# Memory and experts on one core: retrieval by the silu table, its first block in halves, other blocks' sums moved, a sorting router

## The chip, the cores and the metric

The kernel runs on one core of a Trainium2 chip, as one launch. The time is device microseconds from start to end of the execution; the input arrays lie in HBM before it and the output lies there after it.

## What is computed

The input x has 2048 tokens of 128 features, float32. Two sublayers follow, each with a layer norm around it. The first is a memory that is trained by one step and then read; the second is a mixture of eight experts of which each token uses two. Cut to what matters:

```python
def _lmm(params, h):
    for W, b in params:
        h = h + silu(h @ W + b)
    return h

# memory, on x = layernorm(x)
keys, queries, values = x @ Wk + bk, x @ Wq + bq, x @ Wv + bv
alr = 0.1 * sigmoid(x @ Wlr + blr)
grads = grad(sum(mean((_lmm(ps, keys) - values) ** 2, -1) * alr))(((W1, b1), (W2, b2)))
new = p * (1 - LR * WD) - LR * g / (sqrt(g * g) + EPS)
x1 = x0 + layernorm(_lmm(new, queries))

# experts, on y = layernorm(x1)
z = layernorm(y, g, b)
probs = softmax(z @ rW + rb)
w = probs of the top two, divided by their sum
hid = gelu(z @ W1[e] + b1[e])
out = x1 + layernorm(y + sum over e of w[e] * (hid @ W2[e] + b2[e]))
```

## The kernel before

The 2048 tokens are four blocks (NB) of 512, each of four tiles of 128 tokens. Every engine has its own program, written out by hand; they meet only in semaphores. There is no scheduler: the order in the code is the order on each engine.

**Gradients.** Five waves (`wave(w)`) take the blocks through keys, values, the two layers forward and back, and the two weight gradients, which accumulate in PSUM. The last wave also holds the four query products (`q_product`), all of them through PSUM bank 1, with `qT_out` on ScalarE copying each into `qT`. VectorE then makes the new weights and biases (`adam`): first `w2n` together with the biases `bn`, then `w1n`.

**Retrieval** (TensorE `rz1_product`, `rz2_product`, `r_transpose`, `z_transpose`; ScalarE `rsig1_out`, `rsig2_out`, `zT_out`; VectorE `retrieve1`, `retrieve2`, `norm_r`, `residual`, `norm_z`, `z_low`). A layer of the memory is a product, a sigmoid of it by ScalarE (with the bias), then on VectorE a product (matmul + bias) * sigmoid (L903, L911) and a sum with the layer's input (L907, L914). After two layers TensorE transposes the result to token-major form, VectorE takes its statistics, GpSimd the power -0.5 (`rsqrt`, L304), VectorE the residual x1 and the statistics of that, GpSimd two more powers, VectorE the normalised z, TensorE its transposes, and ScalarE the copies `zT` and `z_hi`. `z_hi` is a value in the reduced format that TensorE reads in one pass; `z_lo` is what is left of z, so that a product with three terms is accurate. Blocks 0 to 3 are interleaved; both layers of all four blocks come before the experts, norms only of block 0. Meanwhile `keep_clock` has TensorE transpose the identity into a spare bank 6, 8, 48 and 3 times.

**Experts.** The phase is a loop over slots, -2 to 31; slot m is block m // 8 and expert m % 8. In a slot TensorE makes the hidden products of slot m + 2 (`hidden`, six matmuls of 512 columns) and the output of slot m (`output`, eight matmuls of 128 columns that take two instructions each); ScalarE makes the gelus; VectorE multiplies the output with the router's weight and adds it (`add_expert`, L1063). `due(position, slot)` puts the norms, transposes and router of the next block into fixed slots of the block that runs. `b2_term` is a product of the transposed router weights with the experts' output biases, which GpSimd lays out in `b2_diag` (L320, L324); `start_sum` begins a block's sum with it.

**Router.** `logits` are four small products. VectorE adds the bias and subtracts the maximum (`shift_logits`), ScalarE takes the exponential, and `route` finds the top two by maxima, comparisons and a ramp that settles ties, makes the two weights (`w_tok`), and splits them into a high and a low part (`w_parts`), which `w_transpose` turns.

## Time and profile before

| | |
|---|---|
| Median of 3 runs | 196.87 us (196.78 to 197.1) |
| Profiled execution, own time | 196.74 us |
| Its span, first to last instruction | 194.6 us |
| Mean granted clock of TensorE | 0.984 |
| TensorE busy (matmuls) | 174.4 us, 90% |
| VectorE busy | 147.4 us, 76% |
| ScalarE busy | 102.7 us, 53% |
| GpSimd busy | 25.6 us, 13% |
| Chain that ended last, by engine | TensorE 72%, VectorE 21%, ScalarE 2%, issue 2%, DMA 2% |

The span runs from the first to the last instruction; the 2.1 us around it are the launch and end of the execution. Busy shares are averages over stages. The profile calls TensorE's matmuls PE and its weight loads PEld, VectorE DVE, ScalarE ACT, GpSimd POOL. A granted clock of 1.00 is 2.4 GHz, 0.50 is 1.2 GHz.

### The profile page before, as it was taken

To read this page: it belongs to the slowest core of one execution; us is meant where nothing else is said; L and a number is where in the kernel's file an instruction comes from. 1 tells how busy PE (TensorE), PEld (TensorE's weight loads), DVE (VectorE), ACT (ScalarE), POOL (GpSimd) and SP (SyncE) were. 2 spreads that over 40 slices of the span, in tenths; PEclk is the share of its full clock that TensorE was granted. 3 is DMA by queue.
4 is the path that set the end of the run, shared out by engine and by line. 5 is a ranking of instruction groups with operands and counts; after the bars stand their busy time and mean duration, and the time that the engine had idled before them with its cause. 6 is when DMAs were issued, how large, how long until landed. Compare 5 with 4: busy or idle time off the path is not lost.

```text
span 194.6 us, 3223 instructions
## 1 busy us (share of the span) xinstructions
PE 174.4 (90%) x1085; PEld 142.0 (73%) x1085; DVE 147.4 (76%) x562; ACT 102.7 (53%) x166; POOL 25.6 (13%) x33
## 2 busy tenths in 40 slices
PE   6499999999887994999999899999899999999950
PEld 6344465656543953899999799989789999999950
DVE  1989998997837999797348996568996567557384
ACT  3159768584442167635587336586346595535500
POOL 1450000000000291140000242001142000020011
PEclk9999999999999998899999999999999999999997
DMA  5990000000000000000000000100000100001001
GB/s 162 297 295 18 2 3 0 0 0 3 0 2 0 0 2 3 0 0 0 3 0 2 0 3 0 54 3 0 2 0 3 54 2 0 3 2 54 0 0 54
DMA packets 3423, 4.99 MB, mean 26 GB/s; under 512 B 336, under 2 KB 1744, under 8 KB 3408
## 3 DMA queue, kind: packets, MB, share of 16 engines
q1 hardware_dynamic: 3408, 4.81, 7.8%
q8 instruction: 8, 0.13, 0.3%
q14 instruction: 7, 0.06, 0.1%
HBM read 3.76 MB, written 1.05 MB: 25 GB/s over the span
## 4 chain that ended last, share of the span: by engine, by line
PE 72%; DVE 21%; ACT 2%; issue 2%; DMA 2%; DVEq 0%; ACTq 0%
PE bank L345 65%; PE bank L353 4%; DVE stats L769 3%; DMA x_tok<-in_x_dram 2%; DVE xnT L1063 2%; DVE mv L772 1%; DVE vT L914 1%; DVE s L903 1%; DVE s L911 1%; DVE xnT L907 1%; DVE xn_tok L782 1%; PE bank L476 1%; ACT s L597 1%; PE bank L488 1%; DVE xnT L1074 1%
## 5 line engine op out<-in xcount | busy, mean ns | idle before, releaser
L1063 DVE SCALAR_TENSOR_TENSOR xnT<-bank,w_tok,xnT 128x128 f32<-128x128 f32 x124 | 35.0, 345 | 25.6 <-PE bank L345 25.2
L304 POOL TENSOR_TENSOR rstd<-vpe,minus_half 128x4 f32<-128x4 f32 (+1 forms) x21 | 20.8, 997 | 164.6 <-DVE vpe L777 150.1
L345 PE MATMUL bank<-z_hi,fW_hi 128*128 128x512 f32 x64 | 28.3, 442 | 2.6 <-DVE z_lo L949 2.6
L345 PE MATMUL bank<-z_lo,fW_hi 128*128 128x512 f32 x64 | 25.6, 400 | 0.0
L345 PE MATMUL bank<-z_hi,fW_lo 128*128 128x512 f32 x64 | 25.5, 399 | 0.0
L345 PEld LDWEIGHTS bank<-fW_sb,sig 128*128 128x128 f32 x192 | 23.0, 192 | 0.8
L345 PE MATMUL bank<-fW_sb,sig 128*128 128x128 f32 x192 | 23.2, 275 | 0.0
L708 ACT ACTIVATE sig<-bank,early_sb 128x512 f32<-128x512 f32 x24 | 16.2, 688 | 12.5 <-PE bank L345 12.5
L345 PEld LDWEIGHTS bank<-fW_sb,k_tok 128*128 128x128 f32 x160 | 19.4, 192 | 0.8
L345 PEld LDWEIGHTS bank<-fW_sb,h1T 128*128 128x128 f32 x160 | 19.4, 192 | 0.8
L708 ACT ACTIVATE k_tok<-bank,early_sb 128x512 f32<-128x512 f32 x20 | 13.5, 687 | 12.2 <-PE bank L345 12.1
L345 PE MATMUL bank<-fW_sb,h1T 128*128 128x128 f32 x160 | 19.5, 275 | 0.0
L345 PE MATMUL bank<-fW_sb,k_tok 128*128 128x128 f32 x160 | 19.5, 275 | 0.0
L708 ACT ACTIVATE h1T<-bank,early_sb 128x512 f32<-128x512 f32 x20 | 13.5, 687 | 10.1 <-PE bank L345 10.0
L345 PEld LDWEIGHTS bank<-z_hi,fW_hi 128*128 128x128 f32 x64 | 12.6, 197 | 4.2 <-issue 2.7
L345 PEld LDWEIGHTS bank<-z_lo,fW_hi 128*128 128x128 f32 x64 | 12.3, 192 | 2.8
L424 PEld LDWEIGHTS bank<-ident 128*128 128x128 f32 x93 | 11.7, 153 | 3.1 <-issue 1.6
L424 PE MATMUL bank<-ident 128*128 128x128 f32 x93 | 12.3, 293 | 1.5 <-POOL ident L295 1.5
L345 PEld LDWEIGHTS bank<-z_hi,fW_lo 128*128 128x128 f32 x64 | 12.4, 194 | 1.5
L345 PE MATMUL bank<-xnT,early_sb 128*128 128x512 f32 x24 | 12.0, 596 | 0.8 <-ACT xnT L610 0.8
L597 ACT ACTIVATE s<-bank,bn 128x512 f32<-128x512 f32 x8 | 5.5, 687 | 11.0 <-PE bank L345 11.0
L345 PEld LDWEIGHTS bank<-xnT,early_sb 128*128 128x128 f32 x24 | 4.1, 190 | 3.9 <-issue 3.9
(133 smaller groups left out, 280.7 us busy)
## 6 DMA issues: line engine op xcount, KB each, us to landing
x_tok<-in_x_dram SPq DMA_DIRECT2D x4, 256.0 KB, 4.6
fW_raw<-in_fW_dram SPq DMA_DIRECT2D x1, 1024.0 KB, 9.4
out_dram<-xn_tok SPq DMA_DIRECT2D x3, 256.0 KB, 2.5
early_sb<-in_early_dram SPq DMA_DIRECT2D x1, 268.0 KB, 3.7
late_sb<-in_late_dram SPq DMA_DIRECT2D x1, 264.0 KB, 5.5
b_raw<-in_late_dram SPq DMA_DIRECT2D x16, 4.0 KB
out_dram<-xn_tok SPq DMA_DIRECT2D x2, 128.0 KB, 1.9
fW_sb<-in_fW_dram SPq DMA_DIRECT2D x1, 0.5 KB, 11.9
```

The lines of the kernel that those rows point to most:

```text
L304: pool.tensor_tensor(rstd[:, ln, where], vpe[:, ln, where], minus_half[:, 0:where.stop - where.start], ALU.pow).then_inc(rstd_ready[ln], 1)
L345: return pe.matmul(out_, lhsT, rhs, start=start, stop=stop)
L353: last = pe.transpose(bank[7][:, i * P:(i + 1) * P], pieces(i), ident[:])
L424: pe.transpose(bank[scratch][:, 0:P], ident[:], ident[:])
L476: last = pe.transpose(bank[4][:, i * P:(i + 1) * P], rT[:, b * BLOCK + i * P:b * BLOCK + (i + 1) * P], ident[:])
L488: last = pe.transpose(bank[7][:, i * P:(i + 1) * P], zt_tok[:, t, :], ident[:])
L597: act.activation(cut(into, b), source[:], ACT.Sigmoid, bias=bias).then_inc(s, 1)
L708: act.activation(g_buf[n % G_RING], bank[H_BANK[n % len(H_BANK)]][:], ACT.Gelu, bias=col(FB1 + n % UB)).then_inc(g_done, 1)
L769: last = dve.bn_stats(stats[:, t, :], source(i, t))
L772: last = dve.bn_aggr(mv[:, ln, t, :], stats[:, t, :])
L782: last = dve.tensor_scalar(into[:, t, :], source[:, t, :], mv[:, ln, t, 0:1], scale[:, t:t + 1], ALU.subtract, ALU.mult)
L1063: last = dve.scalar_tensor_tensor(out=y_tok[:, t, :], in0=bank[Y_BANK[m % len(Y_BANK)]][:, i * P:(i + 1) * P], scalar=w_tok[:, t, e:e + 1] ...
```

## The change

**Retrieval.** A layer's activation is one operation on ScalarE, Silu with the bias (`silu1`, `silu2`); VectorE keeps only the sums (`hidden_sum`, `retrieved_sum`). A one-element Silu (`warm`) stands ahead, which brings the table load with it. The retrieval works in five pieces (`RETRIEVED`): two halves of block 0, then blocks 1, 2 and 3. For blocks 1 to 3 the second layer doesn't wait for a sum: TensorE adds the two products w2n * query and w2n * silu in PSUM (`rz2_query`, `rz2_rest`). VectorE's sums for these blocks move into the expert phase, in slots -1, 7 and 15 (`R_SUM`), and with them the norms by two slots or so. Of the `keep_clock` calls behind the gradients only the one with 6 stays.

**Order.** Query products alternate between two banks. Adam makes the biases, `w1n`, then `w2n`. GpSimd builds `b2_diag` as soon as `w1n` is ready, in two operations instead of three. The first two hidden products are made together (`first_hidden`), with the low part of z last; the logits of block 0 follow them.

**Router.** VectorE's max gives the sorted logits of a tile, match_replace marks the top two in a padded copy, and a comparison turns the marks into 0.5 at two places. The weights of a top-two softmax are 0.5 * (1 + tanh((l - other) / 2)); VectorE makes the argument as l minus half the pair's sum, and ScalarE takes Tanh. The exponential, its reductions and the ramp are gone.

The diff, cut to its core:

```diff
         WARM_UP = 28
+        Q_BANK = (1, 2)
...
-        NORM_R, RESIDUAL, NORM_Z, Y_STATS, Y_NORM, Z_LOW, LOGITS_SHIFT, ROUTE = -2, -1, 0, 1, 2, 2, 4, (5, 6)
-        R_TR, Z_TR, LOGITS, EXP, W_TR, B2_TERM = -2, 2, 3, 5, 7, 8
+        R_SUM, NORM_R, RESIDUAL, NORM_Z, Y_STATS, Y_NORM, Z_LOW, CHOOSE, ROUTE = -1, 0, 1, 2, 2, 3, 4, 5, 6
+        R_TR, Z_TR, LOGITS, GATE, W_TR, B2_TERM = 0, 3, 4, 5, 7, 8
...
-        RZ1, RZ2 = (0, 1, 2, 0), (3, 5, 6, 2)
+        RETRIEVED = [(0, HALF), (HALF, HALF)] + [(TB * b, TB) for b in range(1, NB)]
+        RZ1, RZ2 = (3, 5, 7, 5, 6), (6, 2, 3, 2, 6)
+        R_BANK, Z_BANK = (4, 0, 4, 4, 4), (7, 1, 7, 7, 7)
...
+        def piece(tensor, p):
+            return tensor[:, RETRIEVED[p][0] * P:sum(RETRIEVED[p]) * P]
+        def piece_width(p):
+            return RETRIEVED[p][1] * P
...
+            pool.memset(lg[:], NO_MATCH).then_inc(rest_ready, 1)
+            pool.memset(chosen[:], NO_MATCH).then_inc(rest_ready, 1)
             pool.memset(b2_raw[:], 0.0).then_inc(b2_zeroed, 1)
-            rsqrt(LR_, 0)
-            rsqrt(LZ, 0)
-            rsqrt(L1, 0)
             pool.wait_ge(b2_in, 16 * P // E)
+            pool.wait_ge(w1n_ready, 1)
...
+            pool.tensor_tensor(b2_diag[2 * TE:, :], b2_raw[2 * TE:, :], b2_diag[2 * TE:, :].bitcast(F32),
+                               ALU.subtract).then_inc(b2_ready, 1)
+            pool.wait_ge(b2_ready, 1)
...
+            piece_rsqrt(LR_, 0)
+            piece_rsqrt(LR_, 1)
+            piece_rsqrt(LZ, 0)
+            piece_rsqrt(L1, 0)
+            piece_rsqrt(LZ, 1)
+            piece_rsqrt(L1, 1)
...
             def q_product(b):
                 pe.wait_ge(late_in, 16)
-                if b:
-                    pe.wait_ge(qT_ready, b)
-                else:
+                if b == 0:
                     pe.wait_ge(alr_ready, NB)
-                mm(bank[1][:], wq_sb, cut(xnT, b)).then_inc(q_mm, 1)
+                if b == 1:
+                    pe.wait_ge(hv_done, NB)
+                if b >= len(Q_BANK):
+                    pe.wait_ge(qT_ready, b - len(Q_BANK) + 1)
+                mm(bank[Q_BANK[b % len(Q_BANK)]][:], wq_sb, cut(xnT, b)).then_inc(q_mm, 1)
...
+            def rz1_product(p):
+                if p == 0:
                     pe.wait_ge(w1n_ready, 1)
...
+                pe.wait_ge(qT_ready, NB)
+                if p == 3:
+                    pe.wait_ge(rs1_ready, 2)
+                if p == 4:
+                    pe.wait_ge(rs2_ready, 1)
+                mm(bank[RZ1[p]][:, 0:piece_width(p)], w1n[:], piece(qT, p)).then_inc(rz1_mm, 1)
+            def rz2_product(p):
+                if p == 0:
...
+                pe.wait_ge(rh1_done, p + 1)
+                mm(bank[RZ2[p]][:, 0:piece_width(p)], w2n[:], piece(r_h1T, p)).then_inc(rz2_mm, 1)
+            def rz2_query(p):
+                if p == 2:
+                    pe.wait_ge(rs1_ready, 1)
+                if p == 3:
+                    pe.wait_ge(rs2_ready, 2)
+                if p == 4:
+                    pe.wait_ge(rs1_ready, 5)
+                mm(bank[RZ2[p]][:], w2n[:], piece(qT, p), start=True, stop=False)
+            def rz2_rest(p):
+                pe.wait_ge(rs1_ready, p + 1)
+                mm(bank[RZ2[p]][:], w2n[:], piece(r_s1, p), start=False, stop=True).then_inc(rz2_mm, 1)
...
             keep_clock(7, 6)
             rz1_product(0)
-            keep_clock(7, 8)
             rz1_product(1)
+            rz1_product(2)
             rz2_product(0)
-            rz1_product(2)
+            rz2_product(1)
+            rz2_query(2)
             r_transpose(0)
+            r_transpose(1)
             rz1_product(3)
-            keep_clock(7, 48)
-            rz2_product(1)
-            rz2_product(2)
+            rz1_product(4)
+            rz2_query(3)
+            rz2_rest(2)
+            rz2_rest(3)
             z_transpose(0)
-            keep_clock(3, 3)
-            rz2_product(3)
-            logits(0)
+            rz2_query(4)
+            z_transpose(1)
+            rz2_rest(4)
...
+            def first_hidden():
+                pe.wait_ge(x1_ready, 2)
+                pe.wait_ge(zT_ready, 2)
+                for c in range(C):
+                    s = slice(c * P, (c + 1) * P)
+                    mm(bank[H_BANK[c]][:], fW1_hi[:, s], cut(z_hi, 0), start=True, stop=False)
+                    mm(bank[H_BANK[c]][:], fW1_lo[:, s], cut(z_hi, 0), start=False, stop=False)
+                pe.wait_ge(zlo_done, 2)
+                for c in range(C):
+                    mm(bank[H_BANK[c]][:], fW1_hi[:, c * P:(c + 1) * P], cut(z_lo, 0),
+                       start=False, stop=True).then_inc(h_mm, 1)
...
-                if slot + AHEAD < STEPS:
+                if slot == -AHEAD:
+                    first_hidden()
+                    logits(0)
+                elif slot + AHEAD < STEPS:
                     for c in range(C):
                         hidden(C * (slot + AHEAD) + c)
                 if slot == 0:
                     w_transpose(0)
                     pe.wait_ge(fw2_in, 16)
-                    pe.wait_ge(rs2_done, NB)
+                    pe.wait_ge(rs2_ready, len(RETRIEVED))
...
+            def silu1(p):
+                act.wait_ge(rz1_mm, p + 1)
+                if p == 0:
                     act.wait_ge(bn_ready, 1)
                     act.wait_ge(dz1_done, NB)
...
+                act.activation(piece(r_s1, p), bank[RZ1[p]][:, 0:piece_width(p)], ACT.Silu,
+                               bias=bn[:, 0:1]).then_inc(rs1_ready, 1)
+            def silu2(p):
+                act.wait_ge(rz2_mm, p + 1)
+                act.activation(piece(r_s2, p), bank[RZ2[p]][:, 0:piece_width(p)], ACT.Silu,
+                               bias=bn[:, 1:2]).then_inc(rs2_ready, 1)
+            def zT_out(p):
+                act.wait_ge(zt_tr, p + 1)
+                source = bank[Z_BANK[p]][:, 0:piece_width(p)]
+                copy(piece(z_hi, p), source, zhi_done, scale=col(G), bias=col(BB))
+                copy(piece(zT, p), source, zT_ready, scale=col(G), bias=col(BB))
+            def gate_tanh(b):
+                act.wait_ge(gate_in, b + 1)
+                act.activation(tok(gate, b), tok(gate, b), ACT.Tanh).then_inc(gate_ready, 1)
...
-            rsig1_out(0)
-            rsig1_out(1)
-            rsig2_out(0)
-            rsig1_out(2)
-            rsig1_out(3)
-            rsig2_out(1)
-            rsig2_out(2)
+            act.activation(warm[:], minus_half[:, 0:1], ACT.Silu).then_inc(table_ready, 1)
+            silu1(0)
+            silu1(1)
+            silu2(0)
+            silu2(1)
+            silu1(2)
+            silu1(3)
+            silu1(4)
+            silu2(2)
+            silu2(3)
             zT_out(0)
-            rsig2_out(3)
-            exponentials(0)
+            zT_out(1)
+            silu2(4)
...
+                if slot == -1:
+                    gate_tanh(0)
...
-            run(adam(w2n[:], w2_sb, bank[0][:, 0:P], adam_tmp[:, 0, :], adam_tmp[:, 1, :], w2n_ready),
-                adam(bn[:], cols[:, B1:B1 + 2], gbs[:], gb_tmp[:], gb[:, 0, 0:2], bn_ready))
-            dve.wait_ge(w2n_ready, 1)
+            second = adam(w2n[:], w2_sb, bank[0][:, 0:P], adam_tmp[:, 0, :], adam_tmp[:, 1, :], w2n_ready)
+            biases = adam(bn[:], cols[:, B1:B1 + 2], gbs[:], gb_tmp[:], gb[:, 0, 0:2], bn_ready)
+            for _ in range(4):
+                next(second)
+                next(biases)
+            run(biases)
             dve.wait_ge(gw1_mm, 1)
...
+            run(adam(w1n[:], w1_sb, bank[4][:, 0:P], adam_tmp[:, 2, :], adam_tmp[:, 3, :], w1n_ready))
+            run(second)
...
+            def hidden_sum(p):
+                dve.wait_ge(rs1_ready, p + 1)
+                dve.wait_ge(qT_ready, NB)
+                dve.tensor_tensor(piece(r_h1T, p), piece(r_s1, p), piece(qT, p), ALU.add).then_inc(rh1_done, 1)
+            def retrieved_sum(p):
+                dve.wait_ge(rs2_ready, p + 1)
+                dve.wait_ge(rh1_done, p + 1)
+                dve.tensor_tensor(piece(rT, p), piece(r_s2, p), piece(r_h1T, p), ALU.add).then_inc(r_done, 1)
...
-                yield from link(dve.tensor_reduce(small(MX, b), tok(lg, b), AX_X, ALU.max))
-                dve.tensor_tensor(tok(lg, b), tok(lg, b), wide(small(MX, b)),
-                                  ALU.subtract).then_inc(lg_shift, 1)
+                for t in tiles(b):
+                    last = dve.max(ranked[:, t, :], lg[:, t, 0:E])
+                yield from link(last)
+                copied = step(dve.tensor_scalar(chosen[:, span(b), 0:TOP_K], ranked[:, span(b), 0:TOP_K], 1.0, None,
+                                                ALU.mult))
+                yield from link(dve.tensor_tensor(pair_sum[:, span(b)], ranked[:, span(b), 0],
+                                                  ranked[:, span(b), 1], ALU.add))
+                dve.scalar_tensor_tensor(out=tok(gate, b),
+                                         in0=pair_sum[:, span(b)].unsqueeze(2).to_broadcast([P, TB, E]),
+                                         scalar=-0.5, in1=lg[:, span(b), 0:E], op0=ALU.mult,
+                                         op1=ALU.add).then_inc(gate_in, 1)
+                dve.wait_ge(dve_step, copied)
+                for t in tiles(b):
+                    last = dve.match_replace(marked[:, t, :], chosen[:, t, :], lg[:, t, :], -NO_MATCH)
+                yield from link(last)
+                yield from link(dve.tensor_tensor(tok(picked, b), marked[:, span(b), 0:E], lg[:, span(b), 0:E],
+                                                  ALU.is_gt))
+                yield from link(dve.tensor_scalar(tok(picked, b), tok(picked, b), 0.5, None, ALU.mult))
...
-                dve.tensor_tensor(tok(w_tok, b), p, first, ALU.mult).then_inc(w_ready, 1)
+                dve.wait_ge(gate_ready, b + 1)
+                dve.scalar_tensor_tensor(out=tok(w_tok, b), in0=tok(gate, b), scalar=1.0, in1=tok(picked, b),
+                                         op0=ALU.add, op1=ALU.mult).then_inc(w_ready, 1)
...
-            retrieve1(0)
-            retrieve1(1)
-            retrieve2(0)
+            hidden_sum(0)
+            hidden_sum(1)
+            retrieved_sum(0)
+            retrieved_sum(1)
             run(norm_r(0))
-            retrieve1(2)
+            run(norm_r(1))
             run(residual(0))
-            retrieve1(3)
+            run(residual(1))
             norm_z(0)
-            retrieve2(1)
-            retrieve2(2)
-            run(shift_logits(0))
+            norm_z(1)
             z_low(0)
+            z_low(1)
+            run(choose(0))
             run(route(0))
-            retrieve2(3)
...
+                if due(R_SUM, slot):
+                    hidden_sum(due(R_SUM, slot) + 1)
+                    retrieved_sum(due(R_SUM, slot) + 1)
                 if due(NORM_R, slot):
-                    run(norm_r(due(NORM_R, slot)))
...
+                if due(CHOOSE, slot):
+                    run(choose(due(CHOOSE, slot)))
+                if due(ROUTE, slot):
+                    run(route(due(ROUTE, slot)))
```

**TensorE, from the last query product to the first expert product.** Before (`vT` is the retrieved result, `xnT` holds the first layer's sum, `s` its silu, `h_tok` the normalised z, `alrT` z in feature-major form):

```order
L345 MATMUL bank<-xnT,late_sb 128x512 [waits qT_ready,late_in] x2
L424 MATMUL bank<-ident 128x128 x6
L345 MATMUL bank<-qT,w1n 128x512 [waits qT_ready,w1n_ready]
L424 MATMUL bank<-ident 128x128 x8
L345 MATMUL bank<-qT,w1n 128x512 [waits qT_ready]
L345 MATMUL bank<-xnT,w2n 128x512 [waits dh1_done,w2n_ready,rh1_done]
L345 MATMUL bank<-qT,w1n 128x512 [waits hv_done,qT_ready]
L476 MATMUL bank<-ident,vT 128x128 [waits r_done]
...
L424 MATMUL bank<-ident 128x128 x48
L345 MATMUL bank<-xnT,w2n 128x512 [waits rh1_done] x2
L488 MATMUL bank<-ident,h_tok 128x128 [waits dh1_done,zt_ready]
```

The same place with the change:

```order
L372 MATMUL bank<-qT,w1n 128x256 [waits qT_ready,w1n_ready]
L372 MATMUL bank<-qT,w1n 128x256 [waits qT_ready]
L372 MATMUL bank<-qT,w1n 128x512 [waits qT_ready]
L372 MATMUL bank<-xnT,w2n 128x256 [waits rh1_done,dh1_done,w2n_ready]
L372 MATMUL bank<-xnT,w2n 128x256 [waits rh1_done]
L372 MATMUL bank<-qT,w2n 128x512 [waits rs1_ready]
L516 MATMUL bank<-ident,vT 128x128 [waits r_done]
...
L372 MATMUL bank<-s,w2n 128x512 [waits rs1_ready] x2
L525 MATMUL bank<-ident,h_tok 128x128 [waits zt_ready]
L525 MATMUL bank<-ident,h_tok 128x128
L372 MATMUL bank<-qT,w2n 128x512 [waits rs1_ready]
L525 MATMUL bank<-ident,h_tok 128x128 [waits zt_ready]
```

The fillers are gone, the first pieces have 256 columns, and a query product of block 1 or 3 stands ahead of a transpose of block 0.

**VectorE, behind the router of block 0.** Before, one sum of block 3, then block 1's statistics and residual ahead of `start_sum` (L1046):

```order
L911 SCALAR_TENSOR_TENSOR s<-bank,bn,s 128x512
L914 TENSOR_TENSOR vT<-s,xnT 128x512
L769 BN_STATS stats<-bank 128x6 x4
L772 BN_AGGR mv<-stats 128x2 x4
L777 TENSOR_SCALAR vpe<-mv 128x4
L927 SCALAR_TENSOR_TENSOR xn_tok<-bank,rstd,x_tok 128x128 x4
...
L1046 SCALAR_TENSOR_TENSOR xnT<-xn_tok,rstd,bank 128x128 x4
L1063 SCALAR_TENSOR_TENSOR xnT<-bank,w_tok,xnT 128x128 x4
L782 TENSOR_SCALAR h_tok<-xn_tok,mv,rstd 128x128 x4
```

With the change (here at block 1's end, where the same pattern stands for block 2):

```order
L969 TENSOR_TENSOR xnT<-s,qT 128x512
L974 TENSOR_TENSOR vT<-s,xnT 128x512
L1066 SCALAR_TENSOR_TENSOR xnT<-xn_tok,rstd,bank 128x128 x4
L1083 SCALAR_TENSOR_TENSOR xnT<-bank,w_tok,xnT 128x128 x4
L831 BN_STATS stats<-bank 128x6 x4
...
L1083 SCALAR_TENSOR_TENSOR xnT<-bank,w_tok,xnT 128x128 x4
L988 SCALAR_TENSOR_TENSOR xn_tok<-bank,rstd,x_tok 128x128 x4
...
L1083 SCALAR_TENSOR_TENSOR xnT<-bank,w_tok,xnT 128x128 x4
L844 TENSOR_SCALAR h_tok<-xn_tok,mv,rstd 128x128 x4
```

The next block's statistics, residual and normalisation each stand one to three experts later than before, behind `start_sum` instead of ahead of it.

**ScalarE, before the first silu and before the first gelu.** With the change:

```order
L649 ACTIVATE qT<-bank,early_sb 128x512 x3
L753 ACT_TABLE_LOAD
L753 ACTIVATE warm<-minus_half 128x1
L730 ACTIVATE s<-bank,bn 128x256 x2
...
L735 ACTIVATE s<-bank,bn 128x512
L772 ACT_TABLE_LOAD
L772 ACTIVATE sig<-bank,early_sb 128x512 x4
L747 ACTIVATE gate<-gate 128x32
```

One load comes in ahead of the retrieval, and no load stands around `gate`, where two stood around each block's exponential.

## Rows read from the trace of the kernel before

**Rows 1.** The page: busy us, share of the span and instructions.

```profile
PE 174.4 (90%) x1085; PEld 142.0 (73%) x1085; DVE 147.4 (76%) x562; ACT 102.7 (53%) x166; POOL 25.6 (13%) x33
```

**Rows 2.** The chain that ended last: start us, us, what.

```profile
55.98 0.70 ACT s L597
...
58.31 1.14 PE bank L345 x2
59.48 0.70 ACT s L597
...
71.05 1.68 DVE vT L914
...
75.69 2.69 PE bank L345 x6
...
82.10 0.11 PE bank L501
...
186.01 1.14 DVE xnT L1063 x4
```

**Rows 3.** Waits of TensorE from 76 us: us in total, times, longest.

```profile
PE bank L345 <- DVE z_lo L949: 2.6, 1, 2.6
PE bank L501 <- DVE w_parts L1036: 1.7, 2, 0.8
```

**Rows 4.** Stretches: length, busy us (count) by engine, clock, DMA share, GB/s.

```profile
60.00:65.00 5.00, 3.57 (x25) 2.75 (x25) 3.92 (x13) 1.54 (x3) 0.98 (x1) 1.00 0.00 0
...
73.00:74.00 1.00, 0.04 (x1) 0.00 (x0) 0.96 (x2) 0.98 (x2) 0.85 (x1) 1.00 0.00 0
...
75.70:80.00 4.30, 4.30 (x14) 3.48 (x15) 4.03 (x24) 2.18 (x3) 0.00 (x0) 0.60 0.02 4
```

**Rows 5.** Timeline of ScalarE: start us, us, instruction, idle before and its releaser.

```profile
54.39 0.69 ACT L593 ACTIVATE qT<-bank,early_sb 128x512 f32<-128x512 f32 x1 [1.28 <-PE bank L345]
...
100.37 1.28 ACT L686 ACT_TABLE_LOAD   x1
101.66 0.23 ACT L686 ACTIVATE kT<-kT 128x32 f32<-128x32 f32 x1
...
109.39 0.28 ACT L593 ACTIVATE wT<-bank 128x128 fp32r<-128x128 f32 x1 [2.26 <-PE bank L501]
```

**Rows 6.** VectorE: three groups by form (busy us, mean ns), then its timeline.

```profile
L903 DVE SCALAR_TENSOR_TENSOR s<-bank,bn,s 128x512 f32<-128x512 f32 x4 | 3.0, 748 | 2.9 <-ACT s L597 2.8
...
L907 DVE TENSOR_TENSOR xnT<-s,qT 128x512 f32<-128x512 f32 x4 | 2.8, 692 | 0.1
...
L1097 DVE TENSOR_TENSOR xn_tok<-xn_tok,xnT 128x256 f32<-128x256 f32 x2 | 0.9, 426 | 0.1
...
82.93 1.12 DVE L927 SCALAR_TENSOR_TENSOR xn_tok<-bank,rstd,x_tok 128x128 f32<-128x128 f32 x4 [1.19 <-POOL rstd L304]
...
85.66 1.12 DVE L1046 SCALAR_TENSOR_TENSOR xnT<-xn_tok,rstd,bank 128x128 f32<-128x128 f32 x4
...
99.32 0.18 DVE L965 TENSOR_TENSOR kT<-bank,late_sb 128x32 f32<-128x32 f32 x1
99.54 0.19 DVE L969 TENSOR_REDUCE kT<-kT 128x4 f32<-128x32 f32 x1
...
187.89 0.49 DVE L769 BATCH_NORM_STATS2 stats<-xnT 128x6 f32<-128x128 f32 x2
```

**Rows 7.** GpSimd: two groups by form, then its timeline in the tail.

```profile
L304 POOL TENSOR_TENSOR rstd<-vpe,minus_half 128x4 f32<-128x4 f32 x19 | 19.4, 1027 | 150.0 <-DVE vpe L777 135.5 <-DVE vpe L939 14.6
L324 POOL TENSOR_TENSOR b_diag<-b_raw,b_diag 32x512 fp32r<-32x512 f32 x2 | 2.9, 1428 | 0.2
...
188.94 0.70 POOL L304 TENSOR_TENSOR rstd<-vpe,minus_half 128x2 f32<-128x2 f32 x1 [13.75 <-DVE vpe L777]
```

**Rows 8.** Timeline of TensorE: logits, and the next two slots' first products.

```profile
94.01 0.96 PE L345 MATMUL bank<-late_sb,alrT 128*128 128x8 f32 x8
94.82 0.48 PE L345 MATMUL bank<-z_hi,fW_hi 128*128 128x512 f32 x1
...
98.00 0.47 PE L345 MATMUL bank<-z_hi,fW_hi 128*128 128x512 f32 x1
```

285 lines of the change are left out of this document (93 added, 192 removed).

## The prediction

> **What bounds the kernel now.** First the busy shares: TensorE is busy for 174.4 of 194.6 us, VectorE for 147.4 [rows 1]. Then the chain of waits in order of time [rows 2]. From 75.69 us to the last whole-block sum at 186.01 it is nearly all matmuls: the expert phase, 110.3 us. From 55.98 to 75.69 it jumps between ScalarE, VectorE, TensorE and GpSimd: 19.7 us of latency, in which TensorE often just transposes the identity. What ends last there is mostly VectorE, which handles blocks 1 to 3 among the steps of block 0: the sum that starts at 71.05 and takes 1.68 us is a later block's, yet everything of block 0 behind it is late. Last I read what TensorE waits for from 76 us on [rows 3]: 2.6 us for the low part of z (the wait that ends at 75.69) and 1.7 us in two waits for the router weights of blocks 1 and 2. So the change is worth what it takes from the stretch 55.98 to 82.1 (output 0 starts there, behind the transpose of the router weights), plus what it alters in such waits later.
>
> TensorE's clock shows one weak place. In 60 to 65 us it was 1.00 although TensorE idled for 1.43 us of it; from 73 us on TensorE did next to nothing for 2.65 us, and 75.7 to 80 us then ran at 0.60 on average, a stretch at 1.2 GHz instead of 2.4 [rows 4]. That cost 0.4 x 4.3 = 1.7 us.
>
> **The change, step by step.** *Queries.* The last query copy on ScalarE starts at 54.39, after 1.28 us of waiting for its matmul [rows 5], since one PSUM bank serves all four. With two banks I put it at 53.3 and its end at 54.0; both Adam updates are merely reordered and end by then.
>
> *The silu table.* A table load starts at 100.37 and its first user at 101.66 [rows 5]: 1.29 us. With a warm-up activation of 0.2 us the first silu starts at 55.5, where the first sigmoid starts at 55.98 [rows 2]. The Trainium skill speaks against this step: "ScalarE: Activation LUTs", section "What ACT_TABLE_LOAD costs", has each switch end in a drain besides, about 2.66 us in all. By it the sum below would be 2.8 us higher, for two loads on the new path; the row shows no drain.
>
> *Silu itself* has no row. Query copy and sigmoid both take 0.69 us for 512 columns, a copy of 128 columns 0.28 [rows 2, 5]; I take 0.42 for 256, between bounds of 0.28 and 0.69, so -0.3 to +0.5 us for the two on the path.
>
> *Block 0 in halves.* Each layer loses VectorE's product, 0.75 us [rows 6], twice 1.5. The rest goes at half width: VectorE's sum 0.43 [rows 6], 0.47 with its semaphore; from product to activation 59.48 - 58.31 = 1.17 us [rows 2] less half of its 0.86 us of streaming, 0.74. So silu 55.5, sum 56.0, product 56.5, silu 57.2, sum 57.7, transposes 58.2 (the second half's product and block 1's query product stand ahead of them), statistics 58.7.
>
> *Norms.* GpSimd's power takes 1.03 us for four tiles [rows 7] and 0.70 for two, and from the statistics of two tiles to its start there are 188.94 - 187.89 = 1.05 us [rows 6, 7]. The residual step with its statistics takes 85.66 - 82.93 = 2.73 us for four tiles [rows 6]; I take 1.6 for two. So the first power runs 59.7 to 60.4, the residual of half 0 60.5 to 62.1, of half 1 62.1 to 63.7. GpSimd does two powers for half 0 first, so half 1 has its scale at 64.5 and is normalised at 65.15. TensorE is then in a 0.86 us query product until 65.4; the transposes end at 65.85, two ScalarE copies of 0.45 follow, and the **first expert matmul starts at 66.9**. The work of blocks 1 to 3 that left VectorE's queue is what allows this. If it is not out of the way, up to the 1.68 us of one such sum comes back.
>
> *GpSimd's b2 work* (now one operation of 1.43 us [rows 7] behind the copy of 0.7, where two ran) moves ahead, to 53.8 to 56.0, where VectorE idles. If it ends later, the first sums are stretched as the one at 71.05 was, by at most 1.68 - 0.69 = 1.0 us [rows 2, 6].
>
> *To output 0.* The last silu ends at 67.5 and the gelu load at 68.85, so the first gelu is 0.6 us late against its product. Router: logits take 94.82 - 94.01 = 0.81 us of TensorE [rows 8] and are done at 69.3. Chained small VectorE operations follow each other by 99.54 - 99.32 = 0.22 us [rows 6], unchained ones I take at 0.1. Max and match_replace have no row: between nothing and the 0.43 us of a sum of 256 columns [rows 6]; at 8 to 14 columns I take 0.1 and 0.2, nearer the 0.18 us row of 32 columns. Eight per block, 1.2 us: -1.2 to +2.2. The weights are then ready at 72.55; the tanh slips between gelus and, by the instruction order, needs no load. Output 0 starts at 72.75 against 82.1: **-9.3 us**. The clock's 1.7 us are in this gain, but the waits for gelu and router eat most of them.
>
> *In the expert phase.* (a) The transposes of block 1's retrieval now stand behind output 0: **+0.4**. (b) The two waits for router weights, 1.7 us [rows 3], go: the new routing ends over a slot before it is needed, where the old 22 operations had the next block's statistics in their middle. **-1.7**. (c) VectorE gains two sums per block, 1.4 us, and loses about as much routing. It has room on average, but three slots of each block are full: an expert's add is 1.1 us [rows 2], beside it come in slot 0 start_sum and statistics (3.5 in all), in slot 1 the residual (3.8), in slot 2 the normalisation and the output's statistics (3.5), against 98.00 - 94.82 = 3.18 us of TensorE per slot [rows 8]. In block 0 they also begin late, as b2's term comes only in slot 1: start_sum at 76.85, add 78.1, statistics 79.1 to 80.5, power to 81.8, residual to 84.3, power to 85.6, normalised 86.7. TensorE has finished output 3 at 84.6 and stands before block 1's z transposes: a new wait, **+2.1**. For blocks 2 and 3 b2's term comes one slot earlier, and the same count leaves 0.3 us to spare. That thin cover hides it there.
>
> **Sum:** -9.3 + 0.4 - 1.7 + 2.1 = -8.5. The profiled execution took 196.74, so **188.2 us**; the median of the runs, 196.87, is 0.13 above it.
>
> **The rivals.**
>
> 1. *The new wait does not come*, as powers and adds overlap better than I count: 188.2 - 2.1 = 186.1. Against: residual and power depend on each other. 12%.
> 2. *The clock falls once*, in the idle 63.2 to 64.3 of an order that lost its 48 fillers, or in the new wait of 2.1 us. Price as at 75.7: +1.7, 189.9. For: 2.1 is near the 2.65 that preceded the fall. Against: the 1.43 us did nothing [rows 4]. 20%. The Trainium skill ("TensorE: Matmul & The Clock Gate", section "What's actually happening") calls the throttled state the default, which activity releases; by that rule every filler left out is a risk.
> 3. *VectorE binds at each block change*: waits of 2.1 us for blocks 2 and 3 too, 188.2 + 4.2 = 192.4. For: a margin of 0.3 us. 9%.
> 4. *A load holds its user for twice its time*: two loads of 1.29 on the path, +2.6, 190.8. Against: the user at 101.66. 5%. (The skill's drain is of this size.)
> 5. *Slower than before.* The clock falls by 57 us, where the eight fillers between the products are missing, and stays low through the retrieval. The new order has 10.4 us of matmuls there (first layer 3.4; second 6.0, for blocks 1 to 3 in two products each; transposes 0.9); at half clock they are 20.8 and become the path: 54.1 + 20.8 + 2 of latency = 76.9 for the first expert matmul, 1.2 later than before, + 0.4 + 2.1 - 1.7: 196.74 + 2.0 = 198.7. It decides from a fall before 57 us on; one at 64 is rival 2. Against: three products stand back to back there. 4%.
>
> The forecast has 50%, and 187.0 to 189.4 as its own range (silu, small operations, b2's contention).
>
> **The numbers.** A measurement of this kernel tells about 0.2%, 0.4 us, from nothing. All cases but the last are faster by far more: faster 0.96, same 0.01, slower 0.03. The range 185.9 to 191.2 holds the forecast and rivals 1, 2 and 4; rivals 3 and 5 lie outside, 13%.
>
> **What would show it.** First expert matmul at 66 to 68 us; output 0 at about 72.8; TensorE waiting some 2 us for block 1's normalised z at about 85 us and not for router weights; max and match_replace at 0.1 to 0.2 us; clock 1.00 from 60 to 80 us. The mechanism is wrong if the first expert matmul comes after 70 us, if a stretch of the retrieval shows 0.50, or if TensorE idles for more than 4 us in all after output 0.

## The result, and the profile after

The changed kernel takes **188.31 us** (median of 4 runs, 187.76 to 188.97); the kernel before took 196.99 us in the same session (4 runs, 196.78 to 197.2). The ratio is 0.954 (95% interval 0.950 to 0.958). Forecast were 188.2 us and the range 185.9 to 191.2. The profiled execution took 187.79 us, its span is 186.0 us, its mean granted clock 0.99. The four runs are 187.76 and 187.79 (mean clocks 0.993 and 0.990) and 188.82 and 188.97 (0.983 both). Ratios, here and below, leave out runs that lie over 1.5% above the fastest of their kernel.

The page, busy us, share of the span and instructions, to be read against [rows 1]:

```profile
PE 168.9 (91%) x1036; PEld 136.4 (73%) x1036; DVE 137.1 (74%) x541; ACT 95.4 (51%) x165; POOL 25.2 (14%) x36
```

TensorE lost 5.5 us of busy time (fillers, and the 1.7 us of slow clock in [rows 4]), VectorE 10.3 us. The end moved by 8.6 us, so the busy shares hardly changed; what went is waiting, as idle time of TensorE (20.2 us before, 17.1 now) and as the fillers that covered it.

TensorE's timeline, changed kernel (start us, us, instruction, count, and in brackets the idle time before it with its releaser). The places answer to the chain in [rows 2]:

```profile
56.58 1.10 PE L372 MATMUL bank<-xnT,w2n 128*128 128x256 f32 x4 [0.39 <-DVE xnT L969]
...
58.37 0.77 PE L516 MATMUL bank<-ident,vT 128*128 128x128 f32 x4
...
64.49 0.44 PE L525 MATMUL bank<-ident,h_tok 128*128 128x128 f32 x2 [1.05 <-DVE h_tok L844]
...
67.20 0.47 PE L372 MATMUL bank<-z_hi,fW_hi 128*128 128x512 f32 x1 [0.34 <-ACT alrT L649]
...
72.98 0.33 PE L538 MATMUL bank<-ident,w_parts 128*128 128x128 f32 x1 [0.53 <-DVE w_parts L1055]
73.14 1.96 PE L372 MATMUL bank<-fW_sb,sig 128*128 128x128 f32 x16
...
76.75 0.39 PE L372 MATMUL bank<-b_diag,wT 128*128 128x512 f32 x1
...
87.05 0.66 PE L525 MATMUL bank<-ident,h_tok 128*128 128x128 f32 x4 [1.80 <-DVE h_tok L844]
```

The first expert matmul starts at 67.20 (75.69 before), output 0 behind the weights' transpose at 73.14 (82.05 before, in the row below), and one new wait has come, 1.80 us before block 1's z transposes. Output 0 before the change:

```profile
82.05 1.95 PE L345 MATMUL bank<-fW_sb,sig 128*128 128x128 f32 x16
```

The waits of TensorE from 76 us on, to be read against [rows 3] (us in total, times, longest):

```profile
PE bank L525 <- DVE h_tok L844: 1.8, 1, 1.8
```

That is the whole list: no wait for router weights after block 0 and none for blocks 2 and 3. The clock in the stretches that answer to [rows 4] (length, TensorE busy, clock, DMA share, GB/s):

```profile
60.00:65.00 5.00, 3.95 (x12) 1.00 0.00 0
...
75.00:80.00 5.00, 5.00 (x34) 1.00 0.02 3
80.00:88.00 8.00, 6.20 (x47) 1.00 0.00 0
```

ScalarE, against [rows 5]: the load takes as long as the one before and the warm-up starts right at its end, the silus of 256 columns follow each other by 0.41 us:

```profile
53.40 0.69 ACT L649 ACTIVATE qT<-bank,early_sb 128x512 f32<-128x512 f32 x1 [0.17 <-PE bank L372]
54.11 1.28 ACT L753 ACT_TABLE_LOAD   x1
55.40 0.20 ACT L753 ACTIVATE warm<-minus_half 128x1 f32<-128x1 f32 x1
55.51 0.82 ACT L730 ACTIVATE s<-bank,bn 128x256 f32<-128x256 f32 x2
```

VectorE, the new router of block 0, of which [rows 6] had only the small operations around it:

```profile
70.32 0.38 DVE L1024 MAX8 ranked<-lg 128x8 f32<-128x8 f32 x4
...
71.11 0.09 DVE L1036 MATCH_VALUE_LOAD marked<-chosen,lg 128x8 f32 x1
71.18 0.16 DVE L1036 MATCH_REPLACE8 marked<-chosen,lg 128x14 f32<-128x14 f32 x1
71.26 0.08 DVE L1036 MATCH_VALUE_LOAD marked<-chosen,lg 128x8 f32 x1
...
72.70 0.23 DVE L1055 TENSOR_TENSOR w_parts<-w_tok,w_parts 128x64 fp32r<-128x64 f32 x1
...
77.18 1.12 DVE L1066 SCALAR_TENSOR_TENSOR xnT<-xn_tok,rstd,bank 128x128 f32<-128x128 f32 x4 [2.85 <-PE bank L372]
```

A match_replace is two instructions, each pair 0.14 us behind the last. VectorE idles for 2.85 us before `start_sum` (L1066), which needs the product with `b_diag` at 76.75. GpSimd's row of two powers, against [rows 7]:

```profile
59.92 1.52 POOL L325 TENSOR_TENSOR rstd<-vpe,minus_half 128x2 f32<-128x2 f32 x2 [3.77 <-DVE vpe L839]
```

### The profile page after: what moved, and what is told of

It reads as the page before. It is cut to its first block, busy times and chain, and to the rows that moved or that the text cites. A ratio compares the mean times of both kernels' runs of the same rounds, so it can differ in the third digit from the quotient of the medians.

```text
span 186.0 us, 3109 instructions
## 1 busy us (share of the span) xinstructions
PE 168.9 (91%) x1036; PEld 136.4 (73%) x1036; DVE 137.1 (74%) x541; ACT 95.4 (51%) x165; POOL 25.2 (14%) x36
## 4 chain that ended last, share of the span: by engine, by line
PE 72%; DVE 17%; ACT 3%; issue 2%; DMA 2%; POOL 1%; SPq 0%; DVEq 0%; ACTq 0%
PE bank L372 66%; PE bank L380 4%; DVE stats L831 3%; DMA x_tok<-in_x_dram 2%; DVE xnT L1083 2%; DVE mv L834 1%; DVE xn_tok L988 1%; PE bank L525 1%; DVE xn_tok L844 1%; PE bank L516 1%; DVE h_tok L844 1%; ACT L753 1%; DVE xnT L1094 1%; DVE xnT L1114 1%; DVE xnT L1066 1%
## 5 line engine op out<-in xcount | busy, mean ns | idle before, releaser
L325 POOL TENSOR_TENSOR rstd<-vpe,minus_half 128x4 f32<-128x4 f32 (+1 forms) x24 | 21.8, 913 | 116.5 <-DVE vpe L839 105.3
L372 PE MATMUL bank<-z_hi,fW_hi 128*128 128x512 f32 x64 | 27.8, 434 | 0.3 <-ACT alrT L649 0.3
L372 PE MATMUL bank<-z_hi,fW_lo 128*128 128x512 f32 x64 | 25.0, 390 | 0.0
L372 PE MATMUL bank<-z_lo,fW_hi 128*128 128x512 f32 x64 | 25.0, 393 | 0.0
L772 ACT ACTIVATE sig<-bank,early_sb 128x512 f32<-128x512 f32 x24 | 16.1, 687 | 10.5 <-PE bank L372 10.4
L372 PEld LDWEIGHTS bank<-z_hi,fW_hi 128*128 128x128 f32 x64 | 12.1, 189 | 2.5 <-issue 1.1
L372 PEld LDWEIGHTS bank<-z_hi,fW_lo 128*128 128x128 f32 x64 | 12.2, 190 | 1.4
L649 ACT ACTIVATE z_hi<-bank,early_sb 128x512 fp32r<-128x512 f32 (+1 forms) x5 | 3.5, 692 | 7.5 <-PE bank L525 7.4
L1066 DVE SCALAR_TENSOR_TENSOR xnT<-xn_tok,rstd,bank 128x128 f32<-128x128 f32 x16 | 4.5, 343 | 3.5 <-PE bank L372 3.5
L453 PE MATMUL bank<-ident 128*128 128x128 f32 x34 | 5.6, 338 | 1.5 <-POOL ident L316 1.5
```

Of the source, the lines that this page charges most:

```text
L325: pool.tensor_tensor(rstd[:, ln, where], vpe[:, ln, where], minus_half[:, 0:where.stop - where.start], ALU.pow).then_inc(rstd_ready[ln], 1)
L372: return pe.matmul(out_, lhsT, rhs, start=start, stop=stop)
L453: pe.transpose(bank[scratch][:, 0:P], ident[:], ident[:])
L649: act.activation(dst, src, ACT.Identity, **kw).then_inc(s, 1)
L772: act.activation(g_buf[n % G_RING], bank[H_BANK[n % len(H_BANK)]][:], ACT.Gelu, bias=col(FB1 + n % UB)).then_inc(g_done, 1)
L1066: last = dve.scalar_tensor_tensor(out=y_tok[:, t, :], in0=x1_tok[:, t, :], scalar=rstd[:, L1, t:t + 1], in1=bank[B2_BANK][:, i * P:(i + 1) ...
```

## The experiments

Twelve kernels ran, in three batches on three chips, each batch with its own runs of the kernel before. Times are medians; the lowest stands beside them where it says more. The lowest time of the kernel before was 196.78 us beside the changed kernel's first runs and 196.27, 196.69 and 196.75 in the batches, so a difference of up to 0.5 us between two batches says nothing by itself. "Undisturbed" are the runs of a kernel's shortest group, whose mean clock is the higher one.

### The same kernel again, and the new wait

`e1_same` is the changed kernel without an edit; `e2_fill_wait` puts work into the new wait:

```
             def z_transpose(p):
-                pe.wait_ge(zt_ready, p + 1)
                 if p >= 2:
                     pe.wait_ge(zT_ready, p)
                     pe.wait_ge(wT_ready, p - 1)
+                if p == 2:
+                    keep_clock(7, 14)
+                pe.wait_ge(zt_ready, p + 1)
```

`e3_late_ztr` moves block 1's z transposes behind the hidden products of slot 4, ahead of its output, and their copies behind its gelus:

```
+                if slot == 4:
+                    z_transpose(2)
                 if slot >= 0:
                     output(slot)
-                if due(Z_TR, slot):
+                if due(Z_TR, slot) and slot > E:
                     z_transpose(due(Z_TR, slot) + 1)
```

Expected of `e1_same`: 

> The changed kernel again, for the spread: its four runs lay in two groups, 187.8 us at mean clocks of 0.990 and 0.993 and 188.9 at 0.983. Theory: in the runs at 188.9 TensorE's clock falls once, in or behind the new wait of 1.8 us before block 1's z transposes; so again two groups, about 1.1 us apart, the slower one with a mean clock lower by 0.007 to 0.010. Rival: the spread is something else (launch, DMA), and clock and time do not go together.

Expected of `e2_fill_wait`: 

> 14 transposes of the identity (1.5 us) ahead of block 1's z transposes, in the new wait. Theory (the clock falls because TensorE idles there): only the faster group is left, 187.8 us +- 0.2, all mean clocks 0.990 or more. Rival (the spread has another source): both groups stay. If the transposes outlast the wait, up to 0.2 us more.

Expected of `e3_late_ztr`: 

> Block 1's z transposes one step later on TensorE, between the hidden products and the output of slot 4, and their copies on ScalarE behind the gelus of slot 4. Theory: the 1.37 us of hidden products fill the wait, so 0.4 us of 1.8 are left: 187.8 - 1.4 = 186.4, one group only. Rival: the wait moves on to the products that need block 1's z or router weights (slots 6 to 8), and the time stays at 187.8.

Measured: `e1_same` 187.96 us (6 runs: 187.62, 187.63, 187.75, 188.17, 188.83, 189.31; ratio 0.956, 0.952 to 0.960), `e2_fill_wait` 188.26 (187.62 to 189.04, three of six above 188.7; ratio 0.956), `e3_late_ztr` 186.29 (four of six from 186.17 to 186.32, the others 187.64 and 188.87; ratio 0.949, 0.944 to 0.954). So clock and time go together in `e1_same` (0.989 or 0.990 up to 188.17 us, 0.983 and 0.982 in the two above), as expected; the place that was expected, in or behind the new wait, was wrong.

The wait costs time: with `e3` it is 0.42 us in the trace, and the undisturbed runs are 1.4 us shorter, as long as the wait was shortened. The spread of the runs, though, stays in `e2` although TensorE's wait is filled (0.27 us are left in its trace), so it doesn't come from there, and `e3` has long runs too where one group was expected. The trace of `e3`, whose profiled execution was a long one of 188.87 us, shows another place (length, TensorE busy, clock, DMA share, GB/s; the stretch 8 to 12 us of the changed kernel had 2.46 busy at 1.00):

```profile
8.00:12.00 4.00, 2.70 (x6) 0.56 1.02 336
12.00:16.00 4.00, 4.00 (x9) 0.58 0.68 188
```

The clock falls in the opening, where TensorE waits for the first tokens.

### Silu's table left out

`e4_no_silu_table` has no warm-up, and Sigmoid in the place of Silu: the silu function is left out, so the output isn't the reference's. All instructions stay but the load and its user.

```
-            act.activation(warm[:], minus_half[:, 0:1], ACT.Silu).then_inc(table_ready, 1)
...
-               act.activation(piece(r_s1, p), ..., ACT.Silu, bias=bn[:, 0:1])
+               act.activation(piece(r_s1, p), ..., ACT.Sigmoid, bias=bn[:, 0:1])
```

Expected: 

> Sigmoid in place of Silu in the retrieval, so the retrieval's values are another function's; the warm-up and the load of the silu table go. Theory: what ends last before the first silu is then its product, at 54.95 instead of 55.51: 0.5 us less, 187.3 (188.4 in the group with the lower clock), sigmoid and silu at the same 0.41 us for 256 columns. Rival (a load costs a further 1.4 us that the profile hides): 1.9 us less.

Measured: 188.44 us, the lowest 187.66, where `e1_same` had 187.62: neither the 0.5 us that were expected nor the rival's 1.9. Three rows say why, ScalarE's, VectorE's and GpSimd's in `e4` (start us, us, instruction):

```profile
54.80 0.91 ACT L730 ACTIVATE s<-bank,bn 128x256 f32<-128x256 f32 x2 [0.85 <-PE bank L372]
```

```profile
55.30 1.32 DVE L968 TENSOR_TENSOR xnT<-s,qT 128x256 f32<-128x256 f32 x2 [1.23 <-ACT s L730]
```

```profile
54.74 1.26 POOL L341 TENSOR_TENSOR b_diag<-b_raw,b_diag 64x512 fp32r<-64x512 f32 x1
```

The first silu did start 0.71 us earlier (0.15 of it comes from before, as the last Adam step is at 53.78 against 53.93), and so did the first sum. But the first of the two sums alone took 0.99 us instead of 0.43: it ended at 56.29, behind GpSimd's subtraction, which ran to 56.00. Behind it only the 0.15 us are left: the product with `w2n` starts at 56.44 against 56.58. Of the Trainium skill this is the rule in "SBUF — State Buffer", section "Who interferes with whom": a VectorE instruction with two inputs in SBUF and a GpSimd instruction that reads SBUF exclude each other, and the second waits for the first. The rows agree in the main: the sum waited, but it ended 0.29 us behind the subtraction, where a sum by itself takes 0.43. In the changed kernel the sum starts at 56.00, when the subtraction (54.88 to 56.15) is nearly over. The load of silu's table thus stood in a shadow; `e11` and `e12` below take the shadow away as well.

### One part of the change undone at a time

`e5_whole_block` retrieves block 0 in one piece (norms, transposes and waits counted accordingly):

```
-        RETRIEVED = [(0, HALF), (HALF, HALF)] + [(TB * b, TB) for b in range(1, NB)]
+        RETRIEVED = [(TB * b, TB) for b in range(NB)]
```

`e6_sums_early` puts both sums of blocks 1 to 3 back among block 0's norms on VectorE:

```
             run(norm_r(1))
+            hidden_sum(2)
             run(residual(0))
+            hidden_sum(3)
             run(residual(1))
+            hidden_sum(4)
             norm_z(0)
             norm_z(1)
+            retrieved_sum(2)
+            retrieved_sum(3)
```

`e7_old_router` has the router of the kernel before (maxima, ramp, exponential) in the places of the new one:

```
-            run(choose(0))
+            run(shift_logits(0))
             run(route(0))
...
-                act.activation(tok(gate, b), tok(gate, b), ACT.Tanh)
+                act.activation(tok(ex, b), tok(lg, b), ACT.Exp)
```

`e8_no_silu` makes silu as before, a sigmoid by ScalarE and a product by VectorE, ahead of each sum, without the table load:

```
+            def product1(p):
+                dve.wait_ge(rs1_ready, p + 1)
+                dve.scalar_tensor_tensor(out=piece(r_s1, p), in0=bank[RZ1[p]][:, 0:piece_width(p)], scalar=bn[:, 0:1],
+                                         in1=piece(r_s1, p), op0=ALU.add, op1=ALU.mult).then_inc(rs1_done, 1)
```

Expected of `e5_whole_block`: 

> Undoes the halving alone: block 0 in one piece of 512 columns, all else as changed. Theory (the halves shorten a chain of latencies): silu, sum, product, statistics, power, residual, power, normalisation, transposes and copies at full width put the first expert matmul at about 70.2 us instead of 67.2; the gelu load no longer waits, so output 0 is 2.4 to 3.0 us later: 190.5 +- 0.5. Rival (halving doubles instruction overheads and gains nothing): 187.8 +- 0.5.

Expected of `e6_sums_early`: 

> Undoes the move of the sums alone: VectorE makes the six sums of blocks 1 to 3 ahead of the expert phase, one first-layer sum after each of the steps of block 0, two of the second layer before the low part of z. Theory (they stand in VectorE's queue on the path): three sums of 0.69 before block 0's z, first expert matmul 2.0 us later, output 0 too: 189.8 +- 0.4. Rival (VectorE waits for GpSimd's powers anyway and the sums fit in): 187.8 +- 0.3. In the expert phase nothing gets shorter, as the sums there lie in idle time.

Expected of `e7_old_router`: 

> Undoes the router alone: exponential on ScalarE with its two table loads, top two by maxima and the ramp. Theory: in block 0 the chain from logits to weights grows from 2.9 us by about 3.5, output 0 at 76.6; for blocks 1 to 3, with the whole routing in slot 6, TensorE waits about 1 us each for the weights: 187.8 + 3.5 + 3 = 194 +- 1.5. Rival (only block 0's chain counts, VectorE has room later): 191.3.

Expected of `e8_no_silu`: 

> Undoes silu alone: sigmoid by ScalarE and the product (matmul + bias) * sigmoid by VectorE, for all five pieces, in halves for block 0; no silu table. Theory: two products of 0.45 on the path of the first half and the second half's two behind them, three products of 0.75 between the norms, less 0.5 for the table: first expert matmul 3 us later, 190.8 +- 0.7. Rival (the table load eats what the products cost): 187.8 to 188.5.

Measured (the before of this batch 197.07 us):

| | median, lowest | ratio, 95% | first expert matmul | its delay at the start | net of that |
|---|---|---|---|---|---|
| `e5_whole_block` | 191.73, 191.5 | 0.973, 0.967 to 0.979 | 71.25 | 0.98 | +3.1 |
| `e6_sums_early` | 190.51, 190.28 | 0.967, 0.961 to 0.972 | 69.00 | -0.1 | +1.9 |
| `e7_old_router` | 199.66, 199.11 | 1.013, 1.008 to 1.018 | 68.91 | 1.7 | 0.0 |
| `e8_no_silu` | 192.44, 191.15 | 0.975, 0.968 to 0.982 | 73.20 | 2.74 | +3.3 |

The delay at the start is read at the last Adam step of `w2n` (53.93 us in the changed kernel), in `e7` at the first z transposes, and the last column takes it out of the distance to 67.20. It comes from the clock in 8 to 16 us, except for 0.5 us in `e7` and 0.4 in `e8`, by which the first tokens' transposes already start late (8.95 and 8.85 us against 8.46).

*Halves.* `e5` is worth 3.1 us in its trace; with the 1.0 of the start these make 4.1, where 3.9 stand between its profiled execution (191.65) and the changed kernel's. So the expectation holds for the edit, and in the profiled execution 1.0 of the 1.2 us over it belong to the opening; the other runs have no trace.

*Sums.* In `e6` block 0's chain holds three sums of 0.68 us; the first z transposes come at 66.11 instead of 64.49, after a wait of 2.77 us, and behind this longer wait the clock fell (TensorE in `e6`):

```profile
60.00:67.00 7.00, 4.23 (x12) 1.00 0.00 1
67.00:71.00 4.00, 4.00 (x10) 0.57 0.00 0
```

All four runs lie between 190.28 and 191.61, at the least 2.5 above the changed kernel's shortest where 2.0 was expected. The trace has the rest at the slow stretch: the first expert matmul is 1.9 us late net of the start, the weights' transpose 75.47 - 72.98 + 0.1 = 2.6. A long wait didn't always do this: in `e5` TensorE waited nearly as long at the same place and the clock stayed at 1.00 from 60 to 80 us:

```profile
68.96 0.66 PE L518 MATMUL bank<-ident,h_tok 128*128 128x128 f32 x4 [2.53 <-DVE h_tok L830]
```

*Router.* I had expected 194 and missed by 5.7. The router is worth more than any other part, and undoing it alone makes the kernel 1.3% slower than the kernel before. TensorE in `e7`, and then its stretches:

```profile
78.62 0.44 PE L540 MATMUL bank<-ident,w_parts 128*128 128x128 f32 x1 [4.46 <-DVE w_parts L1099]
78.85 3.51 PE L374 MATMUL bank<-fW_sb,sig 128*128 128x128 f32 x16
```

```profile
73.00:79.00 6.00, 1.54 (x8) 0.97 0.00 0
79.00:82.00 3.00, 3.00 (x16) 0.50 0.02 5
```

ScalarE in `e7` loads a table at 73.54 for the exponential and one at 75.08 for the next gelu, 1.28 us each. Against the changed kernel's trace the 12.2 us come from: the start 1.7; the transpose of the weights at 78.62 instead of 72.98, less the start 3.9; output 0 at half clock 1.6 (3.51 for 1.96 us of matmuls); and for each of blocks 1 to 3, from its z transposes to its weights' transpose, 15.66 us instead of 14.06, 1.6 (1.0 of it as a wait of TensorE for `w_parts`), 4.8 in all. These make 12.0. Against the terms that I had expected: 3.9 for 3.5 in block 0, 4.8 for 3 in blocks 1 to 3 (1.6 a block, of which only 1.0 is the wait that I had counted), and no term for the 1.6 of slow clock behind the wait nor for the 1.7 of the start.

*Silu.* The products of VectorE cost 3.3 us net of the start, nearly the same as the halves: `product1` and `product2` stand four times on block 0's chain at 0.48 us, and three of 0.74 us for later blocks stand among its norms. A part of it is again the clock: TensorE waits for 0.80 us before 67.06 and for 0.97 before 69.15, and then runs at half the clock (its stretches in `e8`):

```profile
67.00:71.00 4.00, 2.75 (x6) 0.90 0.00 0
71.00:73.00 2.00, 2.00 (x5) 0.50 0.00 0
```

The first z transposes are 69.15 - 64.49 - 2.74 = 1.9 us late, still at full clock, the first expert matmul 3.3, behind products at half clock. So this edit's own price is not settled better than to 1.9 to 3.3 us.

*Together.* The four prices (3.1, 2.6, 10.5 and 3.3 us net of the start) make over 19 us, where the whole change brings 8.6. They are not shares of the gain: each is what one part costs when it is undone in the new order, with the waits and slow stretches that this brings. The two query banks, the new order of Adam and of `b2_diag`, and the fillers that were left out have not been undone singly.

### What the new wait hangs on, and what the spread of the runs hangs on

`e9_early_b2` moves one matmul:

```
-                if slot == 1:
-                    b2_term(0)
                 if slot >= 0:
                     output(slot)
+                if slot == 0:
+                    b2_term(0)
```

`e10_fill_start` keeps TensorE busy in the opening:

```
-        WARM_UP = 28
+        WARM_UP = 44
             feature_major_x(0)
+            keep_clock(6, 5)
             k_product(0)
             feature_major_x(1)
+            keep_clock(6, 2)
```

`e11_hide_load` moves silu's load into idle time of ScalarE before block 3's last copies, and GpSimd's work on `b2_diag` behind the low parts of z:

```
                     if what in steps:
                         steps[what](b)
+                    if w == NB - 1 and what == "dz1":
+                        act.activation(warm[:], minus_half[:, 0:1], ACT.Silu).then_inc(table_ready, 1)
...
+            pool.wait_ge(zlo_done, 2)
             pool.tensor_scalar(b2_diag[:], b2_raw[:], 1.0, 0.0, ALU.mult, ALU.add).then_inc(b2_high, 1)
```

`e12_all_three` has all of these edits.

Expected of `e9_early_b2`: 

> Edit: the second-layer bias term of block 0 is multiplied right behind output 0 (slot 0) instead of before output 1 (slot 1). My theory of the new wait: block 1's z transposes wait 1.80 us because the residual chain on VectorE is queued behind start_sum, which waits for this one matmul (76.75 us) although the weights it reads are there at 73.3. Then the matmul comes at 75.1, start_sum at about 75.5 instead of 77.18, every later step of the chain about 1.6 earlier, the wait shrinks to at most 0.3 and the faster group of times lies at 186.1 +- 0.3 (1.6 less than 187.7). Rival: the chain is bound by VectorE's own amount of work or by the adds that wait for the outputs (78.44, 80.89), then the wait stays at 1.4 or more and the time at 187.3 to 187.8.

Expected of `e10_fill_start`: 

> Edit: 44 instead of 28 warm-up transposes, 5 more behind the first tokens' transposes and 2 behind the second's, on a free bank. Theory: the two groups of times (187.6 to 187.8, and 188.7 to 189.3) differ in whether TensorE's clock falls to 0.50 in the thin stretch of 8 to 15 us (seen in the profiled runs of e3, e5, e7, e8, not in those of the changed kernel, e1, e2, e4, e6); with TensorE kept busy there, all runs fall in the faster group: 187.7 +- 0.2, clocks of 0.989 and over, at most 1 of 6 runs over 188.5. Rival 1: the fall has nothing to do with the idle time: still about half of the runs over 188.5. Rival 2: the added transposes themselves delay the first tokens: the whole moves up by 0.3 to 0.8.

Expected of `e11_hide_load`: 

> Edit: silu's table is loaded in the idle time of ScalarE before block 3's last copies (about 44.5 us, idle there 1.68), and GpSimd makes the split bias of the second layer only when the low parts of z are done (about 67.6 us) instead of at 54.2. Leaving out silu's load (e4) gained nothing, though the first silu came 0.7 earlier: the first sum on VectorE then took 0.99 instead of 0.43 us, up to the end of GpSimd's subtraction (54.74 to 56.00). Theory: the two hold each other up, as both read two operands from SBUF, so only both edits together gain: first silu at 54.8, first sum at 55.3 taking 0.43, w2n products at 56.2 instead of 56.58, and 187.3 +- 0.2. Rival: the load's place costs nothing and the products wait for their own chain: sum still 0.99 or product still at 56.5, 187.7.

Expected of `e12_all_three`: 

> The edits of e9, e10 and e11 together. If they add up: 1.6 and 0.4 less than 187.7 = 185.7 +- 0.4, in one group of times, ratio to the kernel before 0.944. If only e9's holds: 186.1, with a second group 1.1 to 1.5 above.

Measured (the before of this batch 197.87 us, 11 runs from 196.75 to 200.65):

| | runs, us | ratio, 95% |
|---|---|---|
| `e9_early_b2` | 185.74, 186.05, 187.42, 187.63, 188.65, 188.75 | 0.945, 0.940 to 0.950 |
| `e10_fill_start` | 187.86, 187.86, 188.07, 188.20, 188.22, 188.40 | 0.952, 0.949 to 0.955 |
| `e11_hide_load` | 187.37, 187.51, 188.42, 189.92, 189.94, 190.40 | 0.953, 0.948 to 0.958 |
| `e12_all_three` | 185.57, 185.65, 185.70, 185.77, 185.90 | 0.940, 0.937 to 0.943 |

*The wait.* TensorE and VectorE in `e12`:

```profile
74.35 0.48 PE L371 MATMUL bank<-b_diag,wT 128*128 128x512 f32 x1
...
84.81 0.66 PE L526 MATMUL bank<-ident,h_tok 128*128 128x128 f32 x4
```

```profile
74.87 1.12 DVE L1068 SCALAR_TENSOR_TENSOR xnT<-xn_tok,rstd,bank 128x128 f32<-128x128 f32 x4 [1.05 <-PE bank L371]
```

`start_sum` comes at 74.87 instead of 77.18, and the z transposes have no wait left. The same holds in `e9`, whose trace needs no comparison between batches:

```profile
75.90 1.96 PE L372 MATMUL bank<-fW_sb,sig 128*128 128x128 f32 x16
...
87.99 0.66 PE L525 MATMUL bank<-ident,h_tok 128*128 128x128 f32 x4
```

From output 0 to block 1's z transposes it has 12.09 us, the changed kernel 87.05 - 73.14 = 13.91: 1.82 less, for a wait of 1.80. Its shortest run is 1.9 us under `e1_same`'s; two of its six runs are at the expected 186.1 or below, the others have the longer opening or lie between. So the cause is shown: the new wait was made by one matmul of 0.39 us that stood a slot too late, not by the amount of VectorE's work.

*The spread.* The stretch where TensorE waits for the first tokens, in `e9` (a long execution) and in `e12`:

```profile
8.00:10.00 2.00, 1.11 (x4) 0.67 1.02 330
10.00:12.00 2.00, 1.23 (x2) 0.50 1.06 346
12.00:14.00 2.00, 2.00 (x6) 0.50 0.91 262
```

```profile
8.00:10.00 2.00, 1.77 (x18) 1.00 1.00 325
10.00:12.00 2.00, 1.81 (x9) 1.00 1.08 352
12.00:14.00 2.00, 2.00 (x5) 1.00 0.94 264
```

In `e9` the query copies then run 2.75 us later than in the changed kernel; 0.42 of it is there before the first tokens' transposes (8.88 against 8.46). With the fillers the spread is gone: 0.54 us over six runs of `e10`, 0.33 over five of `e12`, against 1.7 us in `e1` and 3.0 each in `e9` and `e11`, which have no fillers. Rival 1 of this experiment is refuted. The height was missed: 188.13 us where 187.7 +- 0.2 was expected. Whether that is rival 2 can't be told, as the shortest run is only 0.24 us over `e1_same`'s, from another batch, and in `e10`'s trace the last Adam step of `w2n` ends the opening at 53.96 against 53.93. Which fillers do it, the longer warm-up or the seven transposes behind it, wasn't separated.

*The load.* In `e12` silu's load runs at 44.59 us in idle time, the first sums start at 55.56 and take 0.85 for both, and the weights' transpose is at 72.47, 20.44 - 19.82 = 0.62 us nearer to the third query copy than in the changed kernel. In `e11` the distance is the same, 73.42 - 53.60 = 19.82, so the two edits of `e11` gain 0.62 us there, where 0.4 was expected. In the run times it is 0.25 at the least run (187.37 against 187.62, between two batches); the expected 187.3 holds for two of the six runs, the median is 189.17. `e11`'s profiled execution was disturbed twice. Its second fall is behind the new wait itself (TensorE in `e11`):

```profile
84.00:88.00 4.00, 2.13 (x21) 1.00 0.00 0
88.00:92.00 4.00, 4.00 (x19) 0.59 0.00 0
```

Here an idle time of 1.87 us before block 1's z transposes was followed by half the clock from about 88.7 to 92.1 us, at a price of 15.69 - 14.06 = 1.63 us. The profiled executions of the changed kernel, `e1`, `e4` and `e10` had the same wait of 1.80 and kept 1.00.

*Together.* `e12` at 185.70 us is the shortest and steadiest kernel of this study: 0.940 of the kernel before, some 2.0 us under the undisturbed runs of the changed kernel (2.2 between the profiled executions), as expected.

## Why the prediction was right, step by step

**The path to the first expert matmul** was forecast point for point, and its points lie within 0.3 us: last query copy 53.3 (53.40), first silu 55.5 (55.51), first sum 56.0 (56.00), product 56.5 (56.58), second silu 57.2 (57.28), transposes 58.2 (58.37), half 1's residual step ends 63.7 (63.9), expert matmul 66.9 (67.20). The unknown prices fell near the values taken: silu of 256 columns 0.41 (0.42 taken), max 0.10 (0.1), match_replace 0.16 with a load of 0.08 beside it, 0.14 from one to the next (0.2 taken). No drain behind a table load is to be seen in either of the two: 54.11 to 55.40, and 67.66 to 68.95 for the gelu. By the 2.66 us of the Trainium skill ("ScalarE: Activation LUTs", section "What ACT_TABLE_LOAD costs") the time would have been 2.8 us higher; the measurement decides against it.

**Output 0** came at 73.14, 8.9 us earlier instead of 9.3: the router's weights were ready at 72.93, not at 72.55. **The waits for router weights** went entirely, as forecast (1.7). **The new wait** came for block 1 alone, at the time and for the reason given: 87.05 with 1.80 us against 86.7 with 2.1; `e9` shows that the late b2 term was its cause. Blocks 2 and 3 waited for nothing, so the margin of 0.3 us held.

**The sum**: -8.9 + 0.4 - 1.7 + 1.8 = -8.4, and the span fell by 194.6 - 186.0 = 8.6. Between the profiled executions it is 196.74 - 187.79 = 8.95. Most of what is left over lies outside the span: 196.74 - 194.6 = 2.1 us are spent there before, 187.79 - 186.0 = 1.8 after, and nearly all other runs of the two kernels show the same two numbers. The prediction had no term for this 0.3 us; what makes it isn't known.

**What was luck.** The forecast was worked out for a profiled execution, and that one was 0.45 us shorter than forecast, 187.79 for 188.24. The median of 188.31 comes within 0.1 of the forecast because two of the four runs belong to the longer, slower-clocked group, of which the prediction knew nothing; it took 0.4 us as the noise, and the runs span 1.2. Two errors in the terms also pull against each other: 0.4 us too much gain at output 0, 0.3 too much for the new wait. The mechanism and the range don't rest on this.

**The rivals.** Rival 1 is out, as the new wait came. Of rival 2 the places were half right. The clock doesn't fall at 64 us, and behind the new wait it fell in one profiled execution (`e11`). What moves the runs by one to three us is a fall at 8 to 14 us, which the prediction didn't name. The runs of the kernel before spread no less (196.27 to 200.4 in the first batch, with mean clocks of 0.989 at the shortest and 0.978 at 198.2), but no trace shows where. Rival 5, slower by a low clock through the retrieval, came in no trace of the changed kernel. Rivals 3 and 4 are out: 1.3 us of load for its user, and no wait at the later block changes.

**What the parts are worth** was never asked in the prediction, and there my sizes were worse: the old router alone costs 10.5 us net of the start where I expected 6.5. Two terms were short: the idle time of 4.46 us before output 0 was followed by 1.6 us of slow matmuls, which I had at nothing, and each later block costs 1.6 instead of 1.

## What to carry to other kernels

Where a chain of small operations is the bound, write it out step by step with the durations of the nearest rows; here the points so found lay within 0.4 us of the trace over 20 us. For each new wait ask which single instruction it hangs on: here one matmul in a later slot cost 1.8 us, and an earlier place was free. A step that is taken away gains nothing while another engine's work holds the next one up, so look for what ran beside it. And where runs differ by about one per cent, look at the granted clock in the first microseconds: here some fillers where TensorE waits for its first data took away runs that were 1 to 3 us longer, though they made the shortest run no shorter. Before you compare two kernels' medians, see from which group their runs come.

## What was not expected of the hardware

- The opening has two outcomes. TensorE idles before the first tokens' transposes and is then busy for 2.3 to 2.9 of the 4 us from 8 us on. In the profiled executions of the changed kernel, `e1`, `e2`, `e4` and `e6` the clock stayed at 1.00; in `e3`, `e5`, `e7`, `e8`, `e9` and `e11` it went to 0.50, and the later steps came 1.0 to 2.75 us later. The length of the idle time doesn't sort them: 2.13, 0.51, 1.55, 1.74 and 1.45 us where the clock stayed, 2.01, 1.28, 1.50, 2.23, 2.28 and 0.97 us where it fell. With the fillers (`e10`, `e12`), which left no such idle time, it stayed at 1.00 in both.
- In the middle of the kernel the wait of 1.79 or 1.80 us before block 1's z transposes left the clock at 1.00 in eight profiled executions; one of 1.87 us there (`e11`), and before other steps 2.77 us (`e6`), 4.46 us (`e7`), and two of 0.80 and 0.97 close together (`e8`) were followed by 0.50, while 2.53 us in `e5` were not. So the length of the idle time alone doesn't decide it; what does stays open.
- VectorE's sum of 256 columns took 0.99 us instead of 0.43 beside GpSimd's subtraction (`e4`).
- The tanh of the gate needed no table load between two gelus; the exponential of the old router needed two of 1.28 us each (`e7`, at 73.54 and 75.08 us).
